# A state-space scan kernel whose side work is laid out anew over the items of a batch

## Chip, cores and metric

The kernel runs on one core of a Trainium2 chip. The metric is the device time of one execution in microseconds (us), the median of several runs. Engines are named as the profile names them: PE (TensorE), DVE (VectorE), ACT (ScalarE), POOL (GpSimd) and SP (SyncE, which only issues DMAs here).

## What is computed

The reference is a gated block of two parts over `x` of shape 4 x 512 x 512 (batch, time, channel). The first part is a selective state-space model over `ctx` (4 x 512 x 256), gated by the normalised `x`:

```python
x = einsum('bld,ed->bel', ctx, in_proj_w)              # 512 inner channels
x = silu(conv4(x) + conv_b)                            # causal, 4 taps, per channel
dt_low, B, C = split(einsum('bdl,ed->bel', x, x_proj_w), [16, 32])
dt = softplus(einsum('brl,dr->bdl', dt_low, dt_proj_w) + dt_proj_b)
# for each time step, with 16 states n for each channel d:
state = state * exp(dt * A) + (dt * x) * B
y = einsum('bdn,bn->bd', state, C)
y = (y + D * x) * silu(z)                              # z = layernorm of the block's x
x1 = x0 + tanh(g_xattn) * y.T
```

The second part is a layer norm and a mixture of 16 experts with top 2 of them and a shared expert, added to `x1`. The change does not touch it. All data is fp32.

## The kernel before

The scan part handles the four batches one after the other. A batch is 64 **items**: 16 steps `n` (one for each state), each with four groups `j` of 128 channels; item `i = 4n + j`. A batch's steps 0 and 1 stand in the tail of the batch before. A hardware loop runs over the first three batches (`b` = 0, 1, 2); the last batch is written out behind it. Each engine's program is written by hand as a sequence of items with semaphore waits, so the order on an engine is the order in the code, and nothing overtakes.

For each item the engines do the following, in this dependence:

- ACT (`decay`, L1161) writes `dA = exp(dt * A)` for the item into a ring of 8 slots; it may do so when the scan 8 items earlier is over, so ACT can be at most 8 items ahead. At `j == 2` it also writes the four input terms `dbuT` of the step (`input_terms`, L1172).
- PE (`step`, L766) transposes the item's quarter of `dbuT` into one of two PSUM banks `dbu_ps`; it may do so when the scan two items earlier is over, so PE is at most 2 items ahead.
- DVE (`scan`, L1474) runs the recurrence over 512 time steps into `hst`.
- POOL (`products`, L573) multiplies by the broadcast `C` row into `prod`, a ring of 4 slots.
- PE (`add_y`, L784) adds the product of the item five back into `y_ps`.

Between these stand the **pieces**, which prepare the next batch and finish the present one; they are chosen by `(n, j)` in a function `pieces` on each engine. They share two PSUM banks, `mp[0]` and `mp[1]`. Each use of a bank has a number: PE waits in `bank_free(k, use)` until the reader of the use before has counted up `misc_read[k]`, and signals `misc_full[k]`. `LOOP0` and `LOOP1` are the uses of each bank in a loop pass. The pieces are, in order:

- `in_proj` (two 128x512 matmuls into bank 1, for channel groups 3 and 1), whose result DVE folds with four taps (`conv`, L1421 and L1425);
- `conv_proj` (eight 128x512 matmuls for channel groups 0 and 2, the convolution folded into the weights, bank 0), copied by DVE (`conv_to_sbuf`, L1431);
- `z_transposes` (four transposes for one of four time tiles of the present batch's `silu(z)`, bank 0), copied and scaled by ACT (`z_to_time`, L1153);
- `ctx_transposes` of the batch after the next (bank 1), copied by DVE (`ctx_to_sbuf`);
- `silus` on ACT (L1121 and `silu_of_z`, L1114), with an activation table load ahead and one behind;
- `x_proj` (four matmuls, L727), its copy on DVE, `b_transposes` and the store of `C` to DRAM (`store_c` on SP);
- four rounds of `dt_proj` (L741), softplus on ACT (`softplus_parts`), a correction on DVE (`round_part`, L1450) and POOL (`log_part`, L554 and L557), the sum `dt_part` (L1456), `du_part` (L1467), `du_transposes` (L748, bank 1) and ACT's copy `du_to_time` (L1144);
- `post` on DVE at item 6 of the next batch: the gate by `zT`, the residual sum, then statistics (L1483 to L1490).

In the last batch only the z transposes are left as pieces of PE. ACT and DVE there also split the first weights of the second part into high and low halves (L1241, L1598, L1604).

## Time and profile before

| what | value |
|---|---|
| three timed runs | 1126.32, 1129.35, 1129.44 us; median 1129.35 us |
| the profiled execution | 1128.16 us, its span 1126.5 us |
| busy share of the span | PE 82%, PEld 69%, DVE 65%, ACT 54%, POOL 53% |
| mean granted TensorE clock | 0.916 of full |
| scan part | from the start to about 547 us of the span; loop batches of 121.7, 124.6 and 124.3 us from item 0 to item 0, the last batch 105.2 us |
| DMA | 137.08 MB, mean 122 GB/s |

Busy time is the time in which an instruction of the engine ran; a row's idle time is the engine's idle time just before the instructions of that row, put down to what ended it. In a timeline a row stands for one instruction or a run of equal ones (x count), with its start, its length and in brackets the idle time before it. One matmul of 128x512 in fp32 appears as two records. Since matmul records overlap, the pace of PE is read from one start to the next.

### The profile page before, as it was taken

To read this page: it belongs to the slowest core of one execution; us is meant where nothing else is said; L and a number is where in the kernel's file an instruction comes from. 1 tells how busy PE (TensorE), PEld (TensorE's weight loads), DVE (VectorE), ACT (ScalarE), POOL (GpSimd) and SP (SyncE) were. 2 spreads that over 40 slices of the span, in tenths; PEclk is the share of its full clock that TensorE was granted. 3 is DMA by queue.
4 is the path that set the end of the run, shared out by engine and by line. 5 is a ranking of instruction groups with operands and counts; after the bars stand their busy time and mean duration, and the time that the engine had idled before them with its cause. 6 is when DMAs were issued, how large, how long until landed. Compare 5 with 4: busy or idle time off the path is not lost.

```text
span 1126.5 us, 22746 instructions
## 1 busy us (share of the span) xinstructions
PE 926.3 (82%) x5388; PEld 781.1 (69%) x5389; DVE 731.2 (65%) x1023; ACT 613.7 (54%) x1037; POOL 592.3 (53%) x521
## 2 busy tenths in 40 slices
PE   6588977988788877677599989799999999883787
PEld 3266666766666656566489979699898888772676
DVE  4767789877987789599554458445454445444466
ACT  4687997679867987796122213334344445432211
POOL 4556797767966797699210005523434444431164
PEclk9579988998989989899699999989999999995699
DMA  7105111331105113111301015754556656563376
GB/s 250 39 21 186 58 29 39 130 103 31 40 34 184 50 35 108 38 51 35 106 28 47 37 48 168 284 190 162 192 188 228 226 183 227 190 220 112 107 228 236
DMA packets 67432, 137.08 MB, mean 122 GB/s; under 512 B 9392, under 2 KB 15024, under 8 KB 67248
## 3 DMA queue, kind: packets, MB, share of 16 engines
q1 hardware_dynamic: 54736, 105.66, 28.3%
q0 software_dynamic: 8960, 29.37, 7.3%
q10 hardware_dynamic: 3680, 1.39, 0.6%
q8 instruction: 24, 0.39, 0.1%
q14 instruction: 32, 0.26, 0.1%
HBM read 163.53 MB, written 42.07 MB: 183 GB/s over the span
## 4 chain that ended last, share of the span: by engine, by line
PE 39%; issue 4%; DVE 4%; POOL 3%; DMA 1%; ACT 1%; DVEq 0%; ACTq 0%; POOLq 0%
PE psY L955 12%; PE psG L919 11%; PE psU L919 10%; PE psT L912 3%; POOL slot_in L625 3%; PE psHT L933 2%; DVE x_tok L1864 1%; ACT xh L1288 1%; DMA gbuf<-slot_out,posi 0%; DVE hl L1676 0%; PE dbu_ps L766 0%; PE y_ps L784 0%; DVE xl L1682 0%; DVEq L1841 0%; POOL gbuf L672 0%
## 5 line engine op out<-in xcount | busy, mean ns | idle before, releaser
L573 POOL TENSOR_TENSOR prod<-hst,cbc 128x512 f32<-128x512 f32 x256 | 327.8, 1303 | 105.8 <-PE y_ps L784 94.4
L1474 DVE TENSOR_TENSOR_SCAN hst<-dA,dbu_ps 128x512 f32<-128x512 f32 x256 | 302.3, 1206 | 75.6 <-PE dbu_ps L766 57.8
L766 PE MATMUL dbu_ps<-ident,dbuT 128*128 128x128 f32 x1024 | 173.8, 296 | 61.4 <-DVE hst L1474 43.0
L766 PEld LDWEIGHTS dbu_ps<-ident,dbuT 128*128 128x128 f32 x1024 | 127.0, 151 | 127.9 <-DVE hst L1474 82.4
L1161 ACT ACTIVATE dA<-dts,Aneg 128x512 f32 (+1 forms) x256 | 172.6, 713 | 61.1 <-DVE hst L1474 60.4
L1294 ACT CAST hh<-psHT 128x384 fp32r<-128x384 f32 x79 | 37.8, 478 | 287.9 <-PE psHT L933 287.9
L1172 ACT ACTIVATE dbuT<-duT,BT 128x512 f32 (+1 forms) x256 | 163.0, 708 | 1.9 <-PE dbu_ps L766 1.9
L784 PE MATMUL y_ps<-ident,prod 128*128 128x128 f32 x1024 | 161.7, 285 | 1.3 <-POOL prod L573 1.3
L919 PE MATMUL psG<-weights,xh 128*128 (+1 forms) x560 | 140.9, 334 | 15.0 <-issue 8.7
L955 PE MATMUL psY<-weights,hh 128*128 (+3 forms) x420 | 136.3, 406 | 16.8 <-DVE hl L1676 14.6
L919 PE MATMUL psU<-weights,xh 128*128 (+2 forms) x560 | 142.7, 337 | 0.0
L784 PEld LDWEIGHTS y_ps<-ident,prod 128*128 128x128 f32 x1024 | 128.2, 149 | 2.0 <-POOL prod L573 2.0
L919 PEld LDWEIGHTS psG<-weights,xh 128*128 128x128 f32 x560 | 102.5, 195 | 25.2 <-issue 16.7
L660 POOL DMA_DIRECT2D slot_out<-yout x48 | 26.3, 547 | 171.4 <-DVE yout L1697 171.4
L1676 DVE TENSOR_TENSOR hl<-psHT,hh 128x384 fp32r<-128x384 f32 x80 | 44.4, 555 | 99.4 <-ACT hh L1294 99.0
L955 PEld LDWEIGHTS psY<-weights,hh 128*128 128x128 f32 (+1 forms) x420 | 77.6, 192 | 35.6 <-issue 12.1
L919 PEld LDWEIGHTS psU<-weights,xh 128*128 128x128 f32 x560 | 95.8, 191 | 0.0
L919 PE MATMUL psG<-weights,xl 128*128 (+1 forms) x280 | 93.0, 332 | 0.0
L919 PE MATMUL psU<-weights,xl 128*128 (+2 forms) x280 | 91.0, 325 | 0.0
L1241 ACT CAST weights<-raw_gu 128x704 f32 (+1 forms) x76 | 53.9, 778 | 55.8 <-DMA raw_gu<-in_L_ffn_w_gate_up_dram 29.4
L955 PE MATMUL psY<-weights,hl 128*128 (+3 forms) x210 | 83.1, 396 | 0.0
L1697 DVE COPY yout<-psY 128x512 f32<-128x512 f32 x48 | 33.2, 691 | 74.3 <-PE psY L955 65.5
(220 smaller groups left out, 1398.4 us busy)
## 6 DMA issues: line engine op xcount, KB each, us to landing
raw_gu<-in_L_ffn_w_gate_up_dram SPq DMA_DIRECT2D x100, 704.0 KB
raw_d<-in_L_ffn_w_down_dram SPq DMA_DIRECT2D x50, 512.0 KB
cbc<-c_rows SPq DMA_DIRECT2D x64, 256.0 KB, 3.1
slot_in<-ztile SPq DMA_DIRECT2D x3, 4096.0 KB, 13.6
gbuf<-slot_in SPq DMA_DIRECT2D x48, 256.0 KB, 3.1
slot_out<-yout POOLq DMA_DIRECT2D x48, 256.0 KB, 3.2
raw_d<-in_L_ffn_w_down_dram SPq DMA_DIRECT2D x50, 192.0 KB
xn_rows<-xin SPq DMA_DIRECT2D x16, 256.0 KB, 2.0
```

The costliest lines, as they stand in the source:

```text
L573: pool.tensor_tensor(prod[:, prod_slot(n, j), :], hst[:, slot_of(n, j), :], cbc[:, n % 2, :], ALU.mult).then_inc(prod_ready, 1)
L625: pool.indirect_dma_start(slot_in, bass.IndirectOffsetOnAxis(ap=posi[:, c, t:t + 1].bitcast(U32), axis=0), xn_kept_rows[:, t, :], None).th ...
L766: last = tr(dbu_ps[j % 2][:, t * P:(t + 1) * P], dbuT[:, n % 2, t, j * P:(j + 1) * P], ident[:])
L784: last = mm(y_ps[t][:, j * P:(j + 1) * P], prod[:, prod_slot(n, j), t * P:(t + 1) * P], ident[:], start=False, stop=m == ITEMS - 1, is_tra ...
L919: last = mm(ps[:, 0:width], a[:, k, c, :], w_at(w, buf)[:, c, w0:w0 + width], start=n == 0, stop=n == 3 * KH - 1)
L955: last = mm(psY[k][:], a[0:rows, k, c, :], w_at(w, buf)[0:rows, c, :], start=n == 0, stop=n == 8)
L1161: nc.scalar.activation(dA[:, slot_of(n, j), :], par(dts, b)[:, j, :], ACT.Exp, scale=Aneg[:, j, n:n + 1]).then_inc(da_ready, 1)
L1172: last = nc.scalar.activation(dbuT[:, n % 2, t, :], par(duT, b)[:, t, :], ACT.Copy, scale=par(BT, b)[:, t, RK + n:RK + n + 1])
L1241: nc.scalar.copy(dst(wgu_h)[:, c, 0:2 * INTER], raw_gu[:, c, :]).then_inc(gu_hi, 1)
L1294: nc.scalar.copy(hh[:, 1 - k, :, :], psHT[:, 0:3, :]).then_inc(hh_ready, 1)
L1474: V.tensor_tensor_scan(hst[:, slot_of(n, j), :], dA[:, slot_of(n, j), :], dbu_ps[j % 2][:], 0.0, ALU.mult, ALU.add).then_inc(scanned, 1)
L1676: V.tensor_tensor(hl[:, k, :, :], psHT[:, 0:3, :], hh[:, k, :, :].bitcast(F32), ALU.subtract).then_inc(hl_ready, 1)
```

## The change

The pieces get new places, counted in items from the batch's start:

| piece | before | after |
|---|---|---|
| `in_proj`, group 3 | both matmuls at item 9 | one each at 8, 9 |
| `conv_proj`, group 0 | 8 to 15 | 10 to 14, 17 to 19 |
| `in_proj`, group 1 | both at 18 | one each at 15, 16 |
| DVE's taps of group 3; group 1 | 11 to 14; 20 to 23 | 11 to 14; 17, 18, 19, 21 |
| `z_transposes` (PE) | 17, 19, 21, 23 on bank 0 | 23, 25, 27, 29 on bank 1 |
| `z_to_time` (ACT), loop | 24, 26, 28, 30 | 28, 30, 32, 34 |
| `z_transposes`, last batch | 17, 19, 21, 23 | 23, 25, 27, 29 |
| `z_to_time`, last batch | two after 27, two after 31 | 28, 30, 32, 34 |
| `conv_proj`, group 2 | 24 to 31 | 22, 24, 26, 28, 30 to 33 |
| `conv_to_sbuf`, group 0; 2 | 16; 32 | 20; 34 |
| `ctx_transposes`; copies | 32, 34; 33, 35 | 34, 36; 35, 37 |
| `silus` (ACT) | 39, `xs` first, then z | 40, z first, then `xs` |
| `x_proj`; copy on DVE | two each at 37, 38; 39 | one each at 37 to 40; 41 |
| `dt_proj` | 40, 44, 48, 52 | 42, 46, 50, 54 |
| `b_transposes`; copy | 40; 41 | 42; 43 |
| softplus on ACT | 48, 52, 56, 60 | 46, 50, 54, 58 |
| `round_part`; `dt_part`; `du_part` (first of four) | 42; 46; 47 | 44; 48; 49 |
| `log_part` on POOL (first of four) | 42 | 44 |
| `du_transposes` | 49, 53, 57, 61 | 50, 54, 58, 62 |
| `du_to_time` | 58, 62, 64, 65 | 57, 61, 64, 65 |

The uses of the banks change with it, and SP's load of `ctx` waits for bank 1's new count:

```diff
-        LOOP0, LOOP1 = 11, 9
+        LOOP0, LOOP1 = 7, 13
...
-                        sp.wait_ge(misc_full[1], base1(b) + 4)
+                        sp.wait_ge(misc_full[1], base1(b) + 8)
```

The order on PE, and the z transposes' bank:

```diff
             def z_transposes(use, b, t):
-                bank_free(0, use)
+                bank_free(1, use)
...
-                if 2 <= n < 4:
-                    conv_proj(0, base0(b), 0, m)
-                elif 6 <= n < 8:
-                    conv_proj(0, base0(b) + 5, 2, m)
-                if 4 <= n < 6 and j % 2 == 1:
-                    t = n % 2 * 2 + j // 2
-                    z_transposes(base0(b) + 1 + t, b, t)
-                if (n, j) == (2, 1):
-                    in_proj(1, base1(b), 3)
-                if (n, j) == (4, 2):
-                    in_proj(1, base1(b) + 1, 1)
...
+                i = n * ND + j
+                if i in (8, 9):
+                    in_proj(1, base1(b), 3, i - 8)
+                if 10 <= i < 15:
+                    conv_proj(0, base0(b), 0, i - 10)
+                if i in (15, 16):
+                    in_proj(1, base1(b) + 1, 1, i - 15)
+                if 17 <= i < 20:
+                    conv_proj(0, base0(b), 0, i - 12)
+                if i in (22, 24, 26, 28, 30, 31, 32, 33):
+                    conv_proj(0, base0(b) + 1, 2, (i - 22) // 2 if i < 30 else i - 26)
+                if i in (23, 25, 27, 29):
+                    z_transposes(base1(b) + 2 + (i - 23) // 2, b, (i - 23) // 2)
...
+                if 37 <= i < 41:
+                    x_proj(xp_use(bp), bp, i - 37, i - 36)
```

ACT's SiLUs, and its copies in the last batch:

```diff
             def silus(bp, conv_done):
+                silu_of_z(bp)
                 act.wait_ge(*conv_done)
                 nc.scalar.activation(xs[:].rearrange("p j l -> p (j l)"), xs[:].rearrange("p j l -> p (j l)"),
                                      ACT.Silu).then_inc(silu_done, 1)
-                silu_of_z(bp)
...
-                step(NB - 1, n)
-                if 6 <= n < 8:
-                    for t in range(n % 2 * 2, n % 2 * 2 + 2):
-                        z_to_time(NB - 1, t, base0(NB - 1) + t)
+                step(NB - 1, n, z_use=base1(NB - 1))
```

Two places of the built programs show the order. On PE, the loop batch's items 8 and 9 before (`dbu_ps` rows open an item, `mp` rows are its pieces, `winC` is a convolution matmul and `winT` an input projection):

```order
L766 MATMUL dbu_ps<-ident,dbuT 128x128 x4
L782 REGISTER_ALU
L784 MATMUL y_ps<-ident,prod 128x128 x4
L695 ISA
L717 MATMUL mp<-ctxT,winC 128x512
L764 REGISTER_ALU
L766 MATMUL dbu_ps<-ident,dbuT 128x128 x4
L782 REGISTER_ALU
L784 MATMUL y_ps<-ident,prod 128x128 x4
L717 MATMUL mp<-ctxT,winC 128x512
L695 ISA
L707 MATMUL mp<-ctxT,winT 128x512 x2
```

and the same two items now:

```order
L767 MATMUL dbu_ps<-ident,dbuT 128x128 x4
L783 REGISTER_ALU
L785 MATMUL y_ps<-ident,prod 128x128 x4
L695 ISA
L707 MATMUL mp<-ctxT,winT 128x512
L765 REGISTER_ALU
L767 MATMUL dbu_ps<-ident,dbuT 128x128 x4
L783 REGISTER_ALU
L785 MATMUL y_ps<-ident,prod 128x128 x4
L707 MATMUL mp<-ctxT,winT 128x512
```

Item 9 had three large matmuls behind its transposes and has one; the convolution starts two items later. On ACT, the last batch from the decays of step 6 on, before:

```order
L1161 ACTIVATE dA<-dts,Aneg 128x512
L1153 ACTIVATE zT<-mp,tg 128x512 x2
L1161 ACTIVATE dA<-dts,Aneg 128x512 x3
L1172 ACTIVATE dbuT<-duT,BT 128x512 x4
L1161 ACTIVATE dA<-dts,Aneg 128x512
L1153 ACTIVATE zT<-mp,tg 128x512 x2
```

and now:

```order
L1162 ACTIVATE dA<-dts,Aneg 128x512 x2
L1154 ACTIVATE zT<-mp,tg 128x512
L1162 ACTIVATE dA<-dts,Aneg 128x512 x2
L1173 ACTIVATE dbuT<-duT,BT 128x512 x4
L1154 ACTIVATE zT<-mp,tg 128x512
L1162 ACTIVATE dA<-dts,Aneg 128x512 x2
L1154 ACTIVATE zT<-mp,tg 128x512
L1162 ACTIVATE dA<-dts,Aneg 128x512 x2
L1173 ACTIVATE dbuT<-duT,BT 128x512 x4
L1154 ACTIVATE zT<-mp,tg 128x512
```

The two pairs of gate copies are now four single copies, each two items after the other, and PE's transposes for them stand six items later than they did.

## Rows read from the trace of the kernel before

**Rows 1.** The page's costliest groups: busy us, mean ns, idle before and its releaser.

```profile
L573 POOL TENSOR_TENSOR prod<-hst,cbc 128x512 f32<-128x512 f32 x256 | 327.8, 1303 | 105.8 <-PE y_ps L784 94.4
L1474 DVE TENSOR_TENSOR_SCAN hst<-dA,dbu_ps 128x512 f32<-128x512 f32 x256 | 302.3, 1206 | 75.6 <-PE dbu_ps L766 57.8
```

**Rows 2.** Windows: stretch, length, busy (x) of PE, PEld, DVE, ACT, POOL; granted clock, DMA, GB/s.

```profile
72.70:133.70 61.00, 55.01 (x331) 39.13 (x330) 46.09 (x46) 47.38 (x71) 42.92 (x35) 0.97 0.34 113
133.70:181.60 47.90, 36.56 (x222) 30.19 (x221) 40.21 (x37) 40.95 (x69) 43.35 (x33) 0.86 0.11 35
198.30:259.30 61.00, 55.01 (x330) 39.12 (x329) 46.04 (x45) 45.66 (x68) 42.85 (x34) 0.97 0.33 112
259.30:306.30 47.00, 35.50 (x223) 28.80 (x222) 40.55 (x39) 41.03 (x69) 43.18 (x33) 0.89 0.11 35
323.70:383.10 59.40, 53.41 (x331) 38.14 (x330) 46.09 (x46) 45.69 (x68) 42.77 (x34) 1.00 0.34 115
383.10:430.50 47.40, 34.36 (x222) 27.21 (x221) 39.70 (x37) 40.82 (x69) 43.20 (x33) 0.93 0.11 34
447.50:486.40 38.90, 28.41 (x201) 24.77 (x200) 26.72 (x35) 28.29 (x45) 29.28 (x24) 0.87 0.12 35
486.40:537.20 50.80, 37.58 (x275) 30.70 (x273) 47.85 (x41) 38.69 (x63) 47.18 (x36) 0.97 0.13 42
```

**Rows 3.** Timeline of DVE, second loop batch: start, length, instruction, idle before.

```profile
198.28 1.22 DVE L1474 TENSOR_TENSOR_SCAN hst<-dA,dbu_ps 128x512 f32<-128x512 f32 x1
...
207.04 1.21 DVE L1474 TENSOR_TENSOR_SCAN hst<-dA,dbu_ps 128x512 f32<-128x512 f32 x1
...
208.81 1.21 DVE L1474 TENSOR_TENSOR_SCAN hst<-dA,dbu_ps 128x512 f32<-128x512 f32 x1
...
228.03 1.21 DVE L1474 TENSOR_TENSOR_SCAN hst<-dA,dbu_ps 128x512 f32<-128x512 f32 x1
232.03 1.22 DVE L1474 TENSOR_TENSOR_SCAN hst<-dA,dbu_ps 128x512 f32<-128x512 f32 x1 [2.79 <-PE dbu_ps L766]
```

**Rows 4.** Timeline of PE in the same batch, steps 6 and 7.

```profile
229.64 1.50 PE L717 MATMUL mp<-ctxT,winC 128*128 128x512 f32 x2 [2.78 <-ACT zT L1153]
...
235.75 0.60 PE L766 MATMUL dbu_ps<-ident,dbuT 128*128 128x128 f32 x4
...
236.62 1.02 PE L717 MATMUL mp<-ctxT,winC 128*128 128x512 f32 x2
237.49 0.60 PE L766 MATMUL dbu_ps<-ident,dbuT 128*128 128x128 f32 x4
```

**Rows 5.** Timeline of ACT in the same batch, around the SiLUs.

```profile
246.75 1.28 ACT L1121 ACT_TABLE_LOAD   x1
...
249.86 2.91 ACT L1114 ACTIVATE zs<-x_tok,rs 128x512 f32 x4
...
258.39 2.54 ACT L1161 ACTIVATE dA<-dts,Aneg 128x512 f32 x4
```

**Rows 6.** Timelines of PE and DVE in the last batch, steps 4 and 5.

```profile
465.41 1.11 PE L756 MATMUL mp<-ident,zs 128*128 128x128 f32 x4 [4.94 <-ACT zT L1153]
...
467.47 1.22 DVE L1474 TENSOR_TENSOR_SCAN hst<-dA,dbu_ps 128x512 f32<-128x512 f32 x1 [5.75 <-issue]
...
478.42 1.22 DVE L1474 TENSOR_TENSOR_SCAN hst<-dA,dbu_ps 128x512 f32<-128x512 f32 x1 [5.49 <-issue]
```

**Rows 7.** Timeline of ACT in the last batch, steps 8 and 9.

```profile
482.98 2.55 ACT L1172 ACTIVATE dbuT<-duT,BT 128x512 f32<-128x512 f32 x4
...
488.57 2.55 ACT L1172 ACTIVATE dbuT<-duT,BT 128x512 f32<-128x512 f32 x4
```

**Rows 8.** Timelines of POOL and DVE, second loop batch, from step 10 on.

```profile
270.30 5.15 POOL L573 TENSOR_TENSOR prod<-hst,cbc 128x512 f32<-128x512 f32 x4
...
278.81 5.17 POOL L573 TENSOR_TENSOR prod<-hst,cbc 128x512 f32<-128x512 f32 x4
...
300.58 4.54 DVE L1474 TENSOR_TENSOR_SCAN hst<-dA,dbu_ps 128x512 f32<-128x512 f32 x4
```

More of the change, by code:

```diff
@@ L574, in products @@
                                        ALU.mult).then_inc(prod_ready, 1)
-                    if bp is not None and 10 <= n < 14 and j == 2:
-                        log_part(bp, n - 10)
+                    if bp is not None and 11 <= n < 15 and j == 0:
+                        log_part(bp, n - 11)
             for j in range(ND):
@@ L702, in ctx_transposes, with in_proj @@
                 last.then_inc(full, 1)
-            def in_proj(k, use, j):
-                bank_free(k, use)
-                for c in range(NK):
-                    last = mm(mp[k][:], winT[:, c, j * P:(j + 1) * P], ctxT[:, c, PADC:PADC + L],
-                              start=c == 0, stop=c == NK - 1)
-                last.then_inc(misc_full[k], 1)
+            def in_proj(k, use, j, c):
+                if c == 0:
+                    bank_free(k, use)
+                last = mm(mp[k][:], winT[:, c, j * P:(j + 1) * P], ctxT[:, c, PADC:PADC + L],
+                          start=c == 0, stop=c == NK - 1)
+                if c == NK - 1:
+                    last.then_inc(misc_full[k], 1)
             def conv_proj(k, use, j, m):
@@ L755, in z_transposes @@
                 for j in range(ND):
-                    last = tr(mp[0][:, j * P:(j + 1) * P], zs[:, j, t * P:(t + 1) * P], ident[:])
-                last.then_inc(misc_full[0], 1)
+                    last = tr(mp[1][:, j * P:(j + 1) * P], zs[:, j, t * P:(t + 1) * P], ident[:])
+                last.then_inc(misc_full[1], 1)
             def step(b, n, j):
@@ L882, in _ @@
                     add_y(NB - 1, n * ND + j - LAG)
-                    if 4 <= n < 6 and j % 2 == 1:
-                        t = n % 2 * 2 + j // 2
-                        z_transposes(base0(NB - 1) + t, NB - 1, t)
+                    if n * ND + j in (23, 25, 27, 29):
+                        t = (n * ND + j - 23) // 2
+                        z_transposes(base1(NB - 1) + t, NB - 1, t)
             for m in range(ITEMS - LAG, ITEMS):
@@ L1152, in z_to_time @@
                     act.sem_inc(wait_carrier, 1)
-                nc.scalar.activation(zT[:, t, :], mp[0][:], ACT.Copy, scale=tg[:, 0:1]).then_inc(misc_read[0], 1)
+                nc.scalar.activation(zT[:, t, :], mp[1][:], ACT.Copy, scale=tg[:, 0:1]).then_inc(misc_read[1], 1)
             def decay(b, n, j):
@@ L1174, in input_terms, with step @@
                 last.then_inc(dbut_ready, 1)
-            def step(b, n, bp=None):
+            def step(b, n, bp=None, z_use=None):
                 for j in range(ND):
@@ L1182, in step @@
                         pieces(bp, n, j)
+                    t = (n * ND + j - 28) // 2
+                    if z_use is not None and j % 2 == 0 and 0 <= t < NL:
+                        z_to_time(b, t, z_use + t)
             def pieces(bp, n, j):
                 b = bp - 1
-                if 6 <= n < 8 and j % 2 == 0:
-                    t = n % 2 * 2 + j // 2
-                    z_to_time(b, t, base0(b) + 1 + t)
-                if (n, j) == (9, 3):
-                    silus(bp, (misc_read[0], base0(b) + 7))
-                if 12 <= n < 16 and j == 0:
-                    softplus_parts(bp, n - 12)
-                if 14 <= n < 16 and j == 2:
+                i = n * ND + j
+                if i in (28, 30, 32, 34):
+                    t = (i - 28) // 2
+                    z_to_time(b, t, base1(b) + 2 + t)
+                if i == 40:
+                    silus(bp, (misc_read[0], base0(b) + 3))
+                if 11 <= n < 15 and j == 2:
+                    softplus_parts(bp, n - 11)
+                if 14 <= n < 16 and j == 1:
                     du_to_time(bp, n - 14)
```

76 lines of the change are left out of this document (35 added, 41 removed).

## The prediction

> **What bounds the kernel now.** I read the page first: over the span no engine is full, so the share of busy time decides nothing. The costliest groups are POOL's products and DVE's scans, and both idle mostly behind PE [rows 1]. Then I cut the scan part into windows [rows 2]. A loop batch falls into two stretches. In the first, from item 8 to 40 (61.0, 61.0 and 59.4 us), PE is busiest, with 55.0 of 61.0 us, at a granted clock near 1; in the second, from item 40 to the next batch's item 0 (47.9, 47.0 and 47.4 us), POOL is, with 43.2 to 43.4 us. Third, the timelines tell the pace of an item, and the reader is to see three of them.
>
> - PE alone: a new item's transposes start at 235.75, its large matmul at 236.62 and the next item at 237.49 [rows 4]. So transposes and products cost 0.87 us and one large matmul ("a pass") 0.87, 1.74 together. A z or ctx transpose piece is four small transposes, half of that 0.87, so such an item costs 1.31.
> - DVE: a scan alone paces at 1.13 (a run of four is 4.54 long) [rows 8]; with a tap or copy out of PSUM behind it, 1.77, from 207.04 to 208.81 [rows 3].
> - POOL from step 10 on: 8.51 us a step (270.30 to 278.81), 5.15 of it four products, the rest two logarithm corrections [rows 8].
>
> DVE's tap (1.77) hides PE's pass (1.74) in the same item. PE may lead DVE by two items only, so two passes too many in one item aren't absorbed: they are paid in full, while a single pass in an item without DVE work costs 1.74 - 1.13 = 0.61. That is what the new layout plays on. Two real waits stand out besides. In the loop PE waits 2.78 us for ACT's last gate copy before the second convolution (229.64), and runs on at half clock: that matmul row is 1.50 long against 1.02 at full clock [rows 4]. In the last batch PE waits 4.94 us and DVE 5.75 and 5.49 us at two places, for the gate copies again [rows 6]. All four z transposes share a bank with a reader that stands up to ten items further on.
>
> **Part by part.** The working is against the profiled execution, 1128.16 us (1.2 under the median).
>
> *Items 8 to 24, loop.* Before, 198.28 to 228.03, 29.8 us [rows 3]. After: items 8, 9, 10 are PE's, 3 x 1.74 = 5.2; 11 to 14 have a tap each, 4 x 1.77 = 7.1; 15 and 16 (one projection matmul each) 3.3, because the first has to wait for the bank until the tap of item 14; 17 to 21 have DVE work each, 5 x 1.77 = 8.9; 22 and 23 cost 1.13 each, as PE has caught up where item 20 and 21 had none of its work. Sum 26.7, a gain of 3.1. Bounds: 1 (the lead is not regained) to 4.
>
> *Items 24 to 40, loop.* Before, 31.3 us in the second batch. After: 24 and 25 at 1.4 (PE is still a little ahead), 26 to 29 alternate 1.74 and 1.31, 6.1; 30 to 33 are 4 x 1.74 = 7.0; 34 and 35 carry DVE copies, 3.5; 36 costs 1.2. That puts item 37's scan 20.6 us behind item 24's. ACT decides the rest. Its unit costs: four decays or a step's four input terms are 2.55 long as a run and, less the overlap with what follows, 2.45, so 0.61 each; a gate copy is of the same size and taken alike; a table load is 1.28, the load and `xs`'s SiLU 3.11 together (246.75 to 249.86), the z SiLUs 2.9 [rows 5, 7]. Count from the end of scan 20. ACT, eight items ahead, does decay 28 and waits for PE's transposes in item 23, done at 3.3; then until the decay of item 40 stand 12 decays (7.4), three sets of input terms (7.4) and four copies (2.4): 20.5. Load and z SiLUs: 24.7; `xs`'s SiLU (1.83): 26.5. PE wants it for item 37's `x_proj` at about 25.4, so it waits 1 us, scan 38 starts 2.9 behind scan 37, 39 another 1.7. The second table load, two decays and the input terms of step 10 end at 31.4, item 40 follows 2.3 behind 39. Sum 20.6 + 6.9 = 27.5, a gain of 3.8. The half-clock stretch goes with the wait. Bounds: 0 (ACT late by 4 more) to 6 (no wait for the SiLU). The order of the SiLUs alone costs: before, `xs` was ready 3.1 behind its wait, now the z SiLUs come first; only ACT's idle time until the second convolution pays for them.
>
> The Trainium skill ("ScalarE: Activation LUTs", What ACT_TABLE_LOAD costs) counts a switch of sets at about 2.66 us, since it puts a drain of 1.38 behind the load; here load and SiLU of 2048 elements take 3.11 together, and less the load's 1.28 only 1.83 are left for the SiLU itself, so the trace does not agree. By the page both switches would be 1.38 longer, item 40 up to 2.8 later in each loop batch, and the sum below 8 us smaller.
>
> *Item 40 to the next batch, loop.* Everything moves two items back, and the round of one step stays: POOL's 8.51 binds. `round_part` now stands four items nearer the front against ACT's softplus (item 44 against 46, formerly 42 against 48), so its waits for the exponentials go: I price that at 2 to 3 us, the idle time that POOL's rate leaves to be won on DVE (47.0 us against the 43.2 that POOL works). Against it, `log_part` starts two items later (2.3), and the last `du_part` is at item 61: formerly it ended just before the scan of 300.58, and the next batch's first scan came at 306.3, 5.7 us later, through the transposes, ACT's copy, a decay and four input terms [rows 2, 8]. Behind item 61 there are 2 scans of 1.13 to hide it instead of 4, so the chain shows 3.4 us where it showed 1.1. But from the last correction to the end there are two scans fewer, 2.3 us, so that end stays as long as it was. Net I take 46.0 us against 47.4 on the mean, between 45 and 51 (all 2.3 + 2.2 lost, no wait won).
>
> Loop batches: 26.7 + 27.5 + 46.0 = 100.2 against 108.9, 108.0 and 106.8: gains of 8.7, 7.8 and 6.6, together 23.
>
> *Last batch.* The two stalls are DVE's 5.75 and 5.49 [rows 6]. Now PE's transposes at 23 + 2t stand five items ahead of ACT's copy, and the next transposes need ACT past item 28 + 2t, three items ahead of PE: it has six or seven. PE's items alternate between 1.31 and 0.87, 1.09 on the mean, under DVE's 1.13: hidden. So 11.2 us would go; but ACT, which caught up in the stalls, is full: it works 5.59 us a step from step 8 on (482.98 to 488.57) [rows 7] and in the window with the stalls it works 28.3 of 38.9 us, which without 11.2 us of stall is full [rows 2]. Carried on without stalls, its input terms of step 10 come 9 us earlier, not 11. I take 9, bounds 5 and 12.
>
> *Queues passed.* SP's `load_ctx` waits for PE's item 36 instead of 34, with the `C` row of step 10 queued behind it; that row may only be loaded once product 35 is done, which is later, so nothing. `store_c` waits for item 41 instead of 39, ahead of the row of step 12, likewise. The second part starts from DVE's end of the scan part and moves with it.
>
> Sum: 1128.2 - 23 - 9 = 1096. New runs should scatter as the old did, up to 1.2 above the profiled one: **1097**.
>
> **Rivals.**
>
> - *The loop's gain is given back behind item 40.* POOL is the bound there with 43 of 47 us [rows 2]. If the two later items and the longer turn to the next batch are paid in full (4.5 a batch) and the waits for exponentials stay, a loop batch gains 7.8 - 5.9 = 1.9, three of them 6, with the last 15: 1113. For it: POOL has no slack. Against: POOL itself waited for the first correction.
> - *ACT becomes late for bank 1: slower.* The z transposes and ACT's copies now share bank 1, one copy per two items, while ACT also carries decays. Should ACT's lead over PE fall under three items at item 25, PE stands in front of `bank_free`, everything behind it on PE too, and the stalls of the last batch [rows 6] stay there and appear in the loop: 3 x 11.2 = 34 more, against 3 x 4.5 won elsewhere: 1128 + 34 - 13 = 1149. It decides from a lead of three; before, ACT is limited by its ring of eight in most of these items, which speaks against it.
> - *The layout moves passes but their cost stays.* If PE's passes were hidden already wherever they stood, only the last batch gains: 1119. Against: PE's 55 of 61 us.
>
> **How the numbers follow.** Forecast 0.76; given back 0.11; only the last batch 0.05; lost in the noise 0.03 (a measurement of this kernel can tell about 0.3%, 3.4 us); slower 0.05. The forecast's own bounds: loop 3 x (1 + 0 - 3.5) to 3 x (4 + 6 + 2.5), last 5 to 12; taken together and not all at one end, 1084 to 1111. Reaching to the first rival: **1084 to 1115**. Faster 0.92, same 0.03, slower 0.05.
>
> **What would show it.** In the changed profile, items 8 to 24 should take near 27 us and 24 to 40 near 28; no PE wait on `zT` over 1 us; a wait of about 1 us on `xs` before `x_proj`; 46 us behind item 40, with a stall near 3 us before the next batch; the last batch without idle of 5 us on DVE, and ACT full in it. I am wrong if PE waits at `bank_free` for `zT`, if `x_proj` waits over 4 us, or if the windows behind item 40 grow by over 3 us.

## The result and the profile after

The changed kernel takes 1106.42 us on the median of four runs (1105.03 to 1107.3), the kernel before 1127.84 us beside it (1121.5 to 1129.44): the ratio is 0.9826, with a 95% interval from 0.9803 to 0.985. The profiled execution took 1106.53 us, with a span of 1104.9 us against 1126.5. The scan part, from the first scan's start to the last one's end, fell from 475.8 to 453.5 us; all that lies behind it takes 591.4 us instead of 590.8. So the whole gain of the profiled execution, 22.3 us, lies in the scan part.

The page's costliest groups of the kernel after (busy us, mean ns, idle before and its releaser) answer to [rows 1]:

```profile
L573 POOL TENSOR_TENSOR prod<-hst,cbc 128x512 f32<-128x512 f32 x256 | 333.0, 1327 | 84.8 <-PE y_ps L785 66.9
L1476 DVE TENSOR_TENSOR_SCAN hst<-dA,dbu_ps 128x512 f32<-128x512 f32 x256 | 304.0, 1208 | 67.8 <-PE dbu_ps L767 57.8
```

POOL waits 21 us less and DVE 8; POOL's 256 products have themselves become 5.2 us longer in sum. Where the time went is read from the scans' start times on DVE. Each number is the distance between two scans, in the three loop batches one after the other, and the last batch:

| items | before | after | forecast |
|---|---|---|---|
| 0 to 8 | 12.8, 16.7, 17.5; 17.0 | 13.4, 18.2, 16.8; 18.5 | not priced |
| 8 to 24 | 29.8, 29.8, 29.8 | 27.0, 27.0, 27.0 | 26.7 |
| 24 to 40 | 31.2, 31.3, 29.6 | 28.4, 28.4, 28.4 | 27.5 |
| 40 to 44 | 8.5, 9.3, 8.5 | 7.4, 7.4, 7.4 | |
| 44 to 61 | 34.9, 33.1, 34.4 | 33.6, 33.5, 33.7 | |
| 61 to next 0 | 4.5, 4.6, 4.5 | 7.2, 7.2, 7.2 | |
| 40 to next 0 | 47.9, 47.0, 47.5 | 48.1, 48.1, 48.2 | 46.0 |
| last batch, 8 to end | 88.2 | 76.1 | 79.2 |

Items 8 to 40 give 5.6, 5.7 and 4.0 us, 15.2 together; what lies behind item 40 takes back 2.0; the last batch from item 8 on gives 12.2; the items 0 to 8 take back 3.1 (sums taken before rounding). Together that is the 22.3.

The windows of the second and the last batch of the kernel after (length, busy us and instructions of PE, PEld, DVE, ACT, POOL, then the granted clock, the DMA share and GB/s) answer to [rows 2]:

```profile
195.10:222.00 26.90, 26.50 (x163) 18.86 (x162) 24.32 (x25) 17.05 (x27) 21.89 (x18) 1.00 0.44 157
222.00:250.40 28.40, 25.68 (x168) 18.64 (x167) 21.16 (x20) 28.13 (x42) 20.46 (x17) 1.00 0.29 92
250.40:257.80 7.40, 6.82 (x46) 4.55 (x44) 5.51 (x6) 6.23 (x11) 4.59 (x4) 1.00 0.17 40
257.80:291.40 33.60, 24.95 (x160) 20.41 (x161) 30.94 (x30) 30.21 (x51) 33.03 (x25) 0.90 0.09 31
291.40:298.50 7.10, 2.63 (x22) 2.17 (x21) 4.09 (x5) 4.45 (x8) 6.56 (x5) 1.00 0.15 38
...
437.50:466.30 28.80, 25.80 (x204) 21.66 (x203) 27.59 (x36) 26.32 (x43) 28.80 (x24) 1.00 0.15 48
466.30:513.50 47.20, 34.80 (x268) 28.67 (x267) 44.08 (x40) 39.57 (x65) 44.87 (x35) 1.00 0.16 45
```

The stretches now have a nearly full engine, another one each time: PE with 26.50 of 26.9 us in items 8 to 24, ACT with 28.13 of 28.4 in 24 to 40, PE again with 6.82 of 7.4 in 40 to 44, POOL with 33.03 of 33.6 in 44 to 61. The half-clock stretch of [rows 4] is gone: the granted clock is 1.00 from item 8 to 44. In the turn (items 61 to the next 0, the last line of the batch) POOL works 6.56 of 7.1 us, where it worked all of 4.6.

The same cut through the kernel before, second batch, from item 24 on:

```profile
228.00:259.30 31.30, 27.93 (x158) 19.18 (x159) 21.52 (x21) 24.96 (x36) 19.78 (x16) 0.95 0.24 68
259.30:268.60 9.30, 8.14 (x44) 6.14 (x42) 6.21 (x7) 9.27 (x16) 6.05 (x6) 0.82 0.13 32
268.60:301.70 33.10, 24.45 (x156) 20.21 (x156) 30.88 (x29) 27.25 (x46) 32.53 (x24) 0.90 0.09 32
301.70:306.30 4.60, 2.92 (x23) 2.45 (x24) 3.46 (x5) 4.52 (x8) 4.60 (x5) 1.00 0.19 59
```

In items 40 to 44 ACT was full, 9.27 of 9.3 us, and POOL was not. In 44 to 61 POOL was as full as it is now, 32.53 of 33.1 us. The prediction had not cut these lines out, and they decide what lies behind item 40.

### The profile page after: what moved, and what is told of

The parts are those of the page before. It is cut to its first block, busy times and chain, and to the rows that moved or that the text cites. A ratio compares the mean times of both kernels' runs of the same rounds, so it can differ in the third digit from the quotient of the medians.

```text
span 1104.9 us, 22746 instructions
## 1 busy us (share of the span) xinstructions
PE 920.2 (83%) x5388; PEld 776.6 (70%) x5389; DVE 728.1 (66%) x1023; ACT 611.2 (55%) x1037; POOL 594.0 (54%) x521
## 4 chain that ended last, share of the span: by engine, by line
PE 40%; issue 4%; DVE 4%; POOL 3%; DMA 1%; ACT 1%; DVEq 0%; POOLq 0%
PE psY L956 12%; PE psG L920 11%; PE psU L920 10%; PE psT L913 3%; POOL slot_in L625 3%; PE psHT L934 3%; DVE x_tok L1864 1%; ACT xh L1290 1%; DMA gbuf<-slot_out,posi 0%; PE dbu_ps L767 0%; DVE hl L1676 0%; DVEq L1841 0%; DVE xl L1682 0%; PE y_ps L785 0%; POOL gbuf L672 0%
## 5 line engine op out<-in xcount | busy, mean ns | idle before, releaser
L573 POOL TENSOR_TENSOR prod<-hst,cbc 128x512 f32<-128x512 f32 x256 | 333.0, 1327 | 84.8 <-PE y_ps L785 66.9
L767 PE MATMUL dbu_ps<-ident,dbuT 128*128 128x128 f32 x1024 | 169.9, 292 | 38.5 <-ACT dbuT L1173 16.8
L1162 ACT ACTIVATE dA<-dts,Aneg 128x512 f32 (+1 forms) x256 | 169.3, 712 | 33.2 <-DVE hst L1476 32.7
L956 PE MATMUL psY<-weights,hh 128*128 (+3 forms) x420 | 135.7, 405 | 16.7 <-DVE hl L1676 14.3
L1697 DVE COPY yout<-psY 128x512 f32<-128x512 f32 x48 | 33.2, 692 | 73.8 <-PE psY L956 65.8
```

The source lines that it names most:

```text
L573: pool.tensor_tensor(prod[:, prod_slot(n, j), :], hst[:, slot_of(n, j), :], cbc[:, n % 2, :], ALU.mult).then_inc(prod_ready, 1)
L767: last = tr(dbu_ps[j % 2][:, t * P:(t + 1) * P], dbuT[:, n % 2, t, j * P:(j + 1) * P], ident[:])
L956: last = mm(psY[k][:], a[0:rows, k, c, :], w_at(w, buf)[0:rows, c, :], start=n == 0, stop=n == 8)
L1162: nc.scalar.activation(dA[:, slot_of(n, j), :], par(dts, b)[:, j, :], ACT.Exp, scale=Aneg[:, j, n:n + 1]).then_inc(da_ready, 1)
L1697: ins = V.tensor_copy(yout[:, k, :], psY[k][:])
```

## The experiments

All kernels ran beside the kernel before on the same chip. There were three sets: in the first (e1 to e4) that kernel took 1153.12 us, in the second (e5 to e8) 1127.86, in the third (e10, e11 and the changed kernel again) 1149.92. The changed kernel's scan part was 453.5 us in its first profile and 453.6 in the third set, so for it the 22 us more of the third lie behind the scan part; the kernel before was profiled only once. So between sets the stretches are compared, and the ratios within one. The stretches of each kernel come from one profiled execution, and its ratio from four runs, if nothing else is said.

**The changed kernel once more (c_after_again).**

> The changed kernel itself, once more, for the scatter of its stretches. Ratio to before 0.980 to 0.985. If the stretches behind item 40 are set by the order of the program, they come out as in the first look: 24 to 40 28.4, 40 to 64 48.1 us in each loop batch, within 0.3. If the excess of 0.6 to 1.5 us in the items 0 to 8 belongs to the changed kernel (as it would if the longer turn before them were its cause), items 0 to 8 take 13.4, 18.2, 16.8, 18.5 again; if it is scatter from run to run, they differ by a microsecond or more in one batch at least, and need not lie above the 12.8, 16.7, 17.5, 17.0 of before.

Measured: ratio 0.9864 [0.984, 0.9888], above what was expected: 22.3 us of 1149.92 would be 0.981. The scan part has its 453.6 us; what lies behind it took 613.1 us here, and between 613.1 and 619.0 in the three profiles of this set, for the same instructions. That part was not studied, and why it scatters more there is open. Items 8 to 44 came out to 0.1 us (27.0, 28.4, 7.4). Behind item 40 it was 48.5, 48.1 and 51.0: the third is 2.8 longer, so the scatter there is larger than expected. Items 0 to 8 took 12.2, 17.0, 18.5, 17.6, other values in other batches: they don't belong to the changed kernel as such. They go with the granted clock of the stretch. Three windows of items 0 to 8 of the kernel before, then three of the changed one (first profile), show it in the last but two column:

```profile
181.60:198.30 16.70, 11.53 (x83) 10.15 (x82) 16.27 (x21) 14.64 (x24) 10.19 (x11) 0.90 0.10 33
306.30:323.80 17.50, 12.34 (x83) 10.95 (x82) 16.28 (x21) 14.57 (x24) 10.81 (x12) 0.80 0.09 30
430.50:447.50 17.00, 11.83 (x84) 10.45 (x83) 16.27 (x21) 14.65 (x24) 10.25 (x11) 0.90 0.48 158
```

```profile
176.90:195.10 18.20, 13.78 (x83) 12.86 (x82) 16.36 (x21) 14.56 (x24) 10.58 (x11) 0.72 0.09 30
298.50:315.40 16.90, 11.74 (x83) 10.35 (x82) 16.29 (x21) 14.63 (x24) 10.19 (x11) 0.90 0.10 32
419.00:437.50 18.50, 14.08 (x84) 13.16 (x83) 16.47 (x21) 14.57 (x24) 10.79 (x11) 0.72 0.44 145
```

At 0.90 the eight items take 16.7 to 17.0 us, at 0.80 17.5 and at 0.72 18.2 to 18.5, for the same instructions. What makes the clock differ was not tested. In all of them PE first waits 3.5 us for DVE's gates, and DVE then waits for PE; its rows tell at which clock it caught up. The twelve small matmuls before item 8 take 2.35 us in the first of these windows of the changed kernel and 1.55 in the second:

```profile
192.25 2.35 PE L785 MATMUL y_ps<-ident,prod 128*128 128x128 f32 x12
...
313.35 1.55 PE L785 MATMUL y_ps<-ident,prod 128*128 128x128 f32 x12
```

**Only the last batch's gate copies spread (e1_last_only).** The kernel before, with the last batch's z transposes at 23, 25, 27, 29 and copies at 28, 30, 32, 34, still on bank 0:

```diff
-                    if 4 <= n < 6 and j % 2 == 1:
-                        t = n % 2 * 2 + j // 2
+                    if n * ND + j in (23, 25, 27, 29):
+                        t = (n * ND + j - 23) // 2
                         z_transposes(base0(NB - 1) + t, NB - 1, t)
```

> The kernel before, with the new places of the gate transposes (items 23 to 29) and of ACT's four copies (28 to 34) in the last batch alone, on the old bank. If the last batch's part of the change stands by itself, item 8 of that batch to its last scan shortens by 12 us, as it did in the changed kernel (88.2 to 76.1), and the whole run is about 1116; the three loop batches stay at 121.7, 124.6 and 124.3. Rival: that part needs the other bank or comes with the loop's new phase; then it gains under 6 us and the run is above 1121.

Measured: ratio 0.9919 [0.989, 0.9948]. The last batch took 76.2 us from item 8 on, as in the changed kernel, so its 12 us are the spread alone and owe nothing to the bank: over half of the whole gain. The profile shows a second thing: here the loop is the kernel before's, and yet it took 46.1, 46.2 and 46.2 us behind item 40, not 47.9, 47.0 and 47.5. The base from which the prediction reckoned was long by 1.3 us a batch of scatter there (in the first batch items 24 to 40 were 1.4 us longer in turn, 32.6).

**The late pieces put back (e5_late_as_before).** The changed kernel with `x_proj` in pairs at 37 and 38, and `dt_proj`, softplus, corrections, `du_part` and their transposes at their former items:

```diff
-                if 37 <= i < 41:
-                    x_proj(xp_use(bp), bp, i - 37, i - 36)
-                if 10 <= n < 14 and j == 2:
+                if 37 <= i < 39:
+                    x_proj(xp_use(bp), bp, (i - 37) * 2, (i - 36) * 2)
+                if 10 <= n < 14 and j == 0:
...
-                if 12 <= n < 16 and j == 1:
-                    du_part(bp, n - 12)
+                if 11 <= n < 15 and j == 3:
+                    du_part(bp, n - 11)
```

> The changed kernel up to item 36, with everything from x_proj on at the items of the kernel before (x_proj two and two at 37 and 38, dt_proj at 40, softplus at 48, corrections from 42, the last du_part at 59). Theory A: the late pieces' new places lost what the forecast missed behind item 40; then the stretch from 40 stays at 46 to 47.5 us, the turn's idle on DVE is 1.1 instead of 2.9 us, item 40 comes no later than 28.4 us behind item 24 (ACT's input terms set it, not x_proj), and a loop batch is 1 to 3 us shorter than in the changed kernel: ratio to the kernel before 0.974 to 0.980. Rival: doubling x_proj's passes costs what the later places lose, or POOL sets the pace whatever the places; then the batch stays within 1 us of the changed kernel's and the ratio is 0.981 or above.

Measured: ratio 0.9778 [0.9762, 0.9795], the best of its set; the scan part is 448.3 us, 5.2 less than with the whole change. Theory A gave the ratio rightly, but not where: items 24 to 40 went from 28.4 to 29.7, which it had ruled out, and from 40 to the next batch it was 45.6, 45.4 and 45.5 instead of 48.1 (7.9, 33.1 and 4.5 in the three stretches, instead of 7.4, 33.6 and 7.2). The turn made the difference. On DVE, the turn of the changed kernel and then that of this one:

```profile
292.49 0.66 DVE L1469 TENSOR_TENSOR du<-dts,xs 128x512 f32<-128x512 f32 x1
293.07 2.55 DVE L1476 TENSOR_TENSOR_SCAN hst<-dA,dbu_ps 128x512 f32<-128x512 f32 x2
298.52 1.22 DVE L1476 TENSOR_TENSOR_SCAN hst<-dA,dbu_ps 128x512 f32<-128x512 f32 x1 [2.90 <-PE dbu_ps L767]
```

```profile
288.15 0.66 DVE L1469 TENSOR_TENSOR du<-dts,xs 128x512 f32<-128x512 f32 x1
288.74 4.54 DVE L1476 TENSOR_TENSOR_SCAN hst<-dA,dbu_ps 128x512 f32<-128x512 f32 x4
294.42 2.33 DVE L1476 TENSOR_TENSOR_SCAN hst<-dA,dbu_ps 128x512 f32<-128x512 f32 x2 [1.14 <-PE dbu_ps L767]
```

From the last `du` to the next batch's first scan it is 6.0 us with two scans under it and 6.3 with four. The chain is of one length; what counts is how many scans lie over it. Two scans are 2.3 us, and the turn is longer by 2.6.

**`du_part` an item earlier (e2_du_part_early).** Only `du_part` moves, from the second to the first item of its step, to shorten that chain:

```diff
-                if 12 <= n < 16 and j == 1:
+                if 12 <= n < 16 and j == 0:
                     du_part(bp, n - 12)
```

> The changed kernel, with DVE's du_part one item earlier (48, 52, 56, 60, right behind dt_part). Theory A: what the loop lost behind item 40 is PE's wait for du (2.6, 2.0, 2.9 and 1.4 us in a batch), the half clock it leaves behind, and the long chain over the last du at the turn of the batch (2.9 us idle on DVE). Then the stretch from item 40 to the next batch shrinks from 48.1 to about 46.5, the turn's idle from 2.9 to 1.8, and the run is 1100 to 1103. Theory B: POOL's 8.7 us a step binds the stretch; then items 40 to 60 take as long as before and only the turn gains 1.1 a batch or nothing, 1103 to 1106.

Measured: ratio 0.9873 [0.984, 0.9906], against 0.9839 and 0.9824 for the two other edits of its set; the turn fell from 7.2 to 5.5 us, but items 44 to 61 rose from 33.6 to 39.7, 38.4 and 38.4, which neither theory had. DVE's and POOL's rows in this kernel:

```profile
265.69 5.61 POOL L573 TENSOR_TENSOR prod<-hst,cbc 128x512 f32<-128x512 f32 x4
...
268.41 1.75 DVE L1458 TENSOR_TENSOR dts<-sp_r,sp_l 128x512 f32 x1
270.41 1.44 DVE L1469 TENSOR_TENSOR du<-dts,xs 128x512 f32<-128x512 f32 x1 [0.24 <-DVE dts L1458]
...
279.50 1.71 POOL L554 TENSOR_TENSOR sp_t<-sp_t,sp_u 128x512 f32<-128x512 f32 x1
...
278.33 1.76 DVE L1458 TENSOR_TENSOR dts<-sp_r,sp_l 128x512 f32 x1
280.27 1.49 DVE L1469 TENSOR_TENSOR du<-dts,xs 128x512 f32<-128x512 f32 x1 [0.18 <-DVE dts L1458]
```

The same `du` product takes 0.66 us behind a scan and 1.44 here; in all 12 of them 16.8 us against 7.9. These 8.9 us are 3.0 of the 5 us that a batch lost in items 44 to 61 by the move; the rest was not taken apart. In the changed kernel the rows were:

```profile
263.49 5.62 POOL L573 TENSOR_TENSOR prod<-hst,cbc 128x512 f32<-128x512 f32 x4
269.07 1.75 POOL L554 TENSOR_TENSOR sp_t<-sp_t,sp_u 128x512 f32<-128x512 f32 x1
...
269.02 0.66 DVE L1469 TENSOR_TENSOR du<-dts,xs 128x512 f32<-128x512 f32 x1
```

The slow `du` starts 0.89 us before POOL's running product ends (270.41 against 271.30), the fast one 0.09 us before (269.02 against 269.11), and then POOL's next instruction is the long one, 1.75 us. It is so for all of them: the 12 fast ones start 0.1 us before the end of POOL's instruction, and the next one of POOL takes 1.75 to 1.77 us; the 12 slow ones start 0.5 to 0.9 us before it and take 1.06 to 1.50. The Trainium skill ("SBUF — State Buffer", Who interferes with whom) says that a DVE instruction with two SBUF inputs contends with a GpSimd instruction that reads SBUF, and that the order of issue decides which of the two is blocked. The trace agrees: whichever starts second is the longer one.

**The transposes of `du` an item later (e3_du_tr_late).** In the changed kernel PE stood at the `du` transposes for `du_part` in every step, 2.56, 1.97, 2.90 and 1.44 us in the second batch. This edit takes the wait away:

```diff
-                if 12 <= n < 16 and j == 2:
+                if 12 <= n < 16 and j == 3:
                     du_transposes(dut_use(bp) + n - 12, bp, n - 12)
```

> The changed kernel, with PE's transposes of du one item later (51, 55, 59, 63). It takes PE's wait for du away but leaves DVE alone and makes the chain at the turn of the batch one item longer. Theory A, with the turn's chain as the costlier half: the turn's idle grows from 2.9 to 4.0 us, items 44 to 60 gain under 1 us, and the run is 1106 to 1110. Rival: PE's waits and its half clock in items 48 to 60 are what costs; then the stretch from 40 shortens by 1 us or more a batch and the run is 1101 to 1104.

Measured: ratio 0.9839 [0.9814, 0.9865]. Items 44 to 61 stayed at 33.5, 33.5 and 33.5 us though PE no longer waits for `du`, and the turn grew to 7.8, 9.1 and 9.1 us, as theory A had it: the last transposes are on its chain. The three waits in the middle cost nothing: POOL is the bound and PE has slack. The fourth is the turn.

**The former order of the SiLUs (e4_xs_first).** `xs` first, then z:

```diff
-                silu_of_z(bp)
                 act.wait_ge(*conv_done)
...
                                      ACT.Silu).then_inc(silu_done, 1)
+                silu_of_z(bp)
```

> The changed kernel, with ACT's SiLU of xs ahead of the z SiLUs again, as in the kernel before, still at item 40. Theory A (ACT's order matters little, one wait replaces the other): the scan of item 38 comes 1.5 to 2 us earlier, as x_proj no longer waits 1.6 us, and item 40 waits longer for its input terms by 0.5 to 1; a loop batch changes by -1.3 to 0 us and the run is 1103 to 1106. Rival (the new order was needed because ACT has no idle time to give): ACT's wait for the second convolution stands open now, input terms of steps 10 and 11 come over 2 us late, and the run is 1108 or more.

Measured: ratio 0.9824 [0.9802, 0.9845]; items 24 to 40 28.4 us as before the edit. The wait moved and kept its size. In the changed kernel PE waits 1.59 us for `xs` before the first `x_proj`:

```profile
244.58 1.06 PE L728 MATMUL mp<-xs,xpT 128*48 128x512 f32 x2 [1.59 <-ACT xs L1123]
...
246.59 1.06 PE L728 MATMUL mp<-xs,xpT 128*48 128x512 f32 x2
```

and with `xs` first it waits 1.78 us for the input terms of step 10, two items later:

```profile
242.96 1.06 PE L728 MATMUL mp<-xs,xpT 128*48 128x512 f32 x2
...
247.81 0.65 PE L767 MATMUL dbu_ps<-ident,dbuT 128*128 128x128 f32 x4 [1.78 <-ACT dbuT L1173]
```

Scan 38 came 2.01 us behind scan 37 instead of 3.67, scan 40 3.86 behind 39 instead of 2.17. ACT is full, so whichever of its results is asked for first is late.

**Both, the late pieces put back and `xs` first (e10_late_xs_first).** The edits of e5_late_as_before and e4_xs_first together.

> The changed kernel with all that stands from x_proj on where it was before (as in e5_late_as_before) and with xs's SiLU ahead of the z SiLUs. Theory: in e5_late_as_before the 29.7 us of items 24 to 40 hold 1.3 us of waiting for xs, which the pair of x_proj chunks in item 37 pays at once and which nothing behind takes up; with xs ready about 2.9 us earlier that goes until ACT's input terms of step 10 set item 40, as they did in e4_xs_first: 24 to 40 28.4, a loop batch 1.3 shorter, in all 4 us less than e5_late_as_before, ratio 0.974. Rival: the pair of chunks itself costs the 1.3 (two x_proj chunks in one item are more than PE's lead of two items holds), whichever SiLU comes first: 24 to 40 stays at 29.7, ratio 0.978.

Measured: ratio 0.9829 [0.9807, 0.985], 0.9971 of the changed kernel's median on the same chip. Items 24 to 40 fell to 28.4 as the theory had it, but 40 to 44 rose from 7.9 to 8.5, 9.2 and 9.3: in the second and third batch nothing was gained up to item 44, in the first 0.7 us. The theory stopped at item 40, and ACT's work does not. Its table load behind the SiLUs and the row that stands behind the end of DVE's wait for `sp_u` (the next one of the softplus), first with z first, in e5_late_as_before, and then with `xs` first, in e10_late_xs_first:

```profile
241.80 1.28 ACT L1125 ACT_TABLE_LOAD   x1
...
254.71 0.63 ACT L1141 ACTIVATE sp_l<-sp_u 128x512 f32<-128x512 f32 x1
```

```profile
244.13 1.28 ACT L1125 ACT_TABLE_LOAD   x1
...
257.04 0.63 ACT L1141 ACTIVATE sp_l<-sp_u 128x512 f32<-128x512 f32 x1
```

Between the two rows lie 12.91 us in each. Scan 24 started at 219.30 and 221.63, so the load came 22.50 us behind it in both, and the softplus row 35.41. Up to DVE's first correction, in item 42, only what ACT has to do before it counts, and the order of the SiLUs decides merely in which items the same time shows. The correction waits for it on DVE:

```profile
257.04 1.11 DVE L1452 TENSOR_SCALAR sp_t<-sp_u 128x512 f32<-128x512 f32 x1 [1.42 <-ACT sp_u L1139]
```

In the changed kernel the same row of ACT stands 35.44 us behind scan 24, but the correction stands two items later and doesn't wait: items 40 to 44 take 7.4 us. So this late place is worth 1.1 to 1.9 us against e10_late_xs_first. e10_late_xs_first and e5_late_as_before still differ by 0.6 to 1.5 us in 44 to 61, in which nothing was edited; what makes that is open.

**The gate copies three items later (e6_copies_later).** ACT's copies at 31, 33, 35, 37 instead of 28, 30, 32, 34:

```diff
-                if i in (28, 30, 32, 34):
-                    t = (i - 28) // 2
+                if i in (31, 33, 35, 37):
+                    t = (i - 31) // 2
```

> The changed kernel, with ACT's four gate copies three items later, at 31, 33, 35, 37 in every batch; PE's transposes stay. It tests from which distance the shared bank bites. PE at item 25 + 2t then needs ACT past item 31 + 2t, six items ahead, where it was three. Theory A: it bites at that distance: PE waits over 0.5 us for zT at two or three of the transposes and before the first ctx transpose, items 24 to 40 grow from 28.4 to 31 or more, and the last batch gets its stalls back (76.1 us from item 8 becomes 80 or more); ratio 0.990 to 1.005. Rival: ACT's lead of eight covers it; all stretches within 0.5 us, ratio about 0.983.

Measured: ratio 0.9889 [0.9869, 0.9909] (two runs only), just under the range of theory A. Items 24 to 40 took 29.3 instead of 28.4 us, the last batch from item 8 on 81.5 instead of 76.1, and PE stands in front of the bank again. The waits on `zT` in the whole program, in this kernel (who waited, us, times), and in the changed one:

```profile
  PEld mp L757: 13.0, 8
  POOL dA L580: 11.2, 4
  PE mp L757: 11.1, 8
```

```profile
  PEld mp L757: 1.1, 1
  DVE dA L1556: 0.9, 1
  PE mp L757: 0.9, 1
```

This is the mechanism of the rival that ended slower. The copies at five items' distance are clear of it, those at eight are not, and even then it costs 10.5 us of the scan part (464.0 against 453.5), not the 34 that the rival gave it: the loop pays 0.9 us a batch in 24 to 40, up to 2.9 behind 40, where the unchanged program scattered by 2.8, and 5.4 in the last batch. No kernel put the z transposes of the loop back to their old items or bank, so how the gain of items 24 to 40 divides between those two is not shown.

**`in_proj` in pairs again (e7_in_proj_doubled).** Both matmuls of a pair at item 9 and at 16 (the second edit is like the first):

```diff
-                if i in (8, 9):
-                    in_proj(1, base1(b), 3, i - 8)
+                if i == 9:
+                    in_proj(1, base1(b), 3, 0)
+                    in_proj(1, base1(b), 3, 1)
```

> The changed kernel, with both matmuls of each input projection in one item again (9 and 16), and none in 8 and 15. Theory A (a pass alone costs 1.74 - 1.13 = 0.61 us, a second one in the same item its full 0.87, since PE leads by two items only): items 8 to 24 take 27.5 us instead of 27.0, three times, 1.5 us in all, which only the trace can tell. Rival: PE's lead takes it up, and the stretch stays at 27.0 or falls.

Measured: ratio 0.9799 [0.978, 0.9819] (two runs only); items 8 to 24 26.8 us instead of 27.0: the rival held. Item 8 takes 1.14 and item 9 2.33 us where both took 1.73, item 15 1.13 and 16 2.14. The sums are 3.47 against 3.46 and 3.27 against 3.47: a pair in one item, with a free one ahead, costs what two single ones cost. PE's lead of two items takes it up. So spreading the two matmuls of a pair did not bring the 2.8 us of this stretch. What differs from the kernel before is that there item 9 held three passes, the pair and one of the convolution, and took 3.45 us, and that three z transposes, at 17, 19 and 21, stood among the taps. No kernel divides the gain between the two, but the scans' distances in the second batch do by place: 1.6 us of it lie in items 8 to 16, all in item 9, and 1.2 in 17 to 23.

**The turn filled (e8_turn_filled).** ACT's last `du_to_time` of a batch behind the decay of item 2 of the next batch instead of ahead of it (the old call at `j == 1` goes, which is not shown):

```diff
                     decay(b, n, j)
+                    if j == 2 and n == 0 and bp is not None:
+                        du_to_time(bp, 3)
                     if j == 2:
                         input_terms(b, n)
```

> The changed kernel, with ACT's last du_to_time of a batch behind the decay of item 2 of the next batch instead of ahead of it, so that this decay runs while ACT waits for PE. Theory A: the chain du_part, PE's transposes, ACT's copy, input terms, PE's transposes sets the next batch's item 0, and the decay stands in it with 0.6 us: DVE's idle at the turn falls from 2.9 to 2.3 us, 1.8 us in all, more if PE keeps its clock. Rival: something else (POOL's products) sets that item; then it doesn't move.

Measured: ratio 0.9802 [0.9784, 0.982]; the turn 7.0 instead of 7.2 us, a third of the 0.6 expected. The stall on DVE fell from 2.90 to 2.70. That decay was mostly not on the chain.

**All together (e11_best).** e10_late_xs_first, with `in_proj` in pairs and the turn filled.

> All that has helped or cost nothing, together: e10_late_xs_first, with each projection matmul pair of in_proj in one item again (9 and 16), and du_to_time(3) put between the scans of the next batch's items 1 and 2. Theory: pieces add, so loop batches take 27.0 to 26.8 us in items 8 to 24, 28.4 in 24 to 40, 45.3 in 40 to 64; ratio 0.973 to 0.975. Rival: e7_in_proj_doubled's 0.2 us came only because slack followed, and moving the copy at the turn pushes du_to_time behind the scan that ACT's decay chain waits for, now that the turn has only 1.1 us of stall: the turn grows by about 0.6 us a batch and the ratio is that of e10_late_xs_first or 0.001 to 0.002 above it.

Measured (six runs): ratio 0.9782 [0.9751, 0.9812], 0.9915 of the changed kernel's median on the same chip; the scan part 448.7 us, against 448.3 of e5_late_as_before. Stretches 26.8, 28.4, then 47.3, 47.2 and 46.8 behind item 40. Neither the theory's 45.3 behind item 40 nor the rival's longer turn came (it fell to 4.4). It does not beat e5_late_as_before (0.9778 in its own set); both are ahead of the changed kernel, by under 1%.

## Why the prediction was right, and where not

The forecast was 1097 us with a range from 1084 to 1115; measured 1106.42. Direction and places held; the loop's gain was overrated: 13.2 us from item 8 on instead of 23. That the total still came within 10 us owes something to luck: the last batch gave 3.2 us more than forecast, and items 0 to 8, which stood in no sum, took 3.1.

- **Items 8 to 24: right in the sum.** 26.7 forecast, 27.0 measured. Items 8 to 10 at 1.73 each and those with a tap at 1.77 are the paces of [rows 3, 4]. The rule given, that two passes too many in an item are paid in full, stands for item 9 of before (three passes, 3.45 us); for a pair alone it does not: e7_in_proj_doubled shows that it costs nothing with a free item ahead of it.
- **Items 24 to 40: right in mechanism, 0.9 us short.** Scan 37 came 20.55 us behind scan 24 (forecast 20.6). Then 3.67, 2.01 and 2.17 instead of 2.9, 1.7 and 2.3. The wait for `xs` was 1.59 us instead of 1, and an item with `x_proj` takes 2.01 us and not 1.74: `x_proj`'s two rows lie 2.01 apart. ACT is the bound, as the forecast said, and e4_xs_first and e10_late_xs_first show that the order of its SiLUs only moves the wait.
- **Item 40 to the next batch: the step that failed.** Forecast 46.0, measured 48.1, three times 2.1. Both terms were seen, the waits and the turn, and their sum was wrong.
  - The waits. "Its waits for the exponentials go" came true: DVE waited 1.15, 1.50 and 0.34 us for `sp_u` in the second batch before (in all 3.0; 3.9 and 4.7 in the two others), and never in the changed kernel. They were priced at 2 to 3 us, out of the distance between 47.0 and POOL's 43.2. That idle time of POOL lay ahead of item 44. There the first of the waits was indeed worth something: items 40 to 44 take 7.4 us instead of 8.5, 9.3 and 8.5, and e10_late_xs_first, with the correction at its old item, has 8.5 to 9.3 again. The later waits lay in items 44 to 61, where POOL was full already, and were worth nothing: e5_late_as_before has them again (1.0 to 1.7 us in item 46) and takes 33.0 to 33.2 us there against 33.6.
  - The turn. 3.4 us of stall were forecast and 2.90 measured, but "that end stays as long as it was" took it out of the sum again. It was paid in full: the turn is 7.2 us instead of 4.5, and with the pieces at their old items (e5_late_as_before) 4.5 again. The prediction let the same two scans, 2.3 us, pay both for the later `log_part` and for the longer chain. Its terms as they stand, 2 to 3 us won, 2.3 and 2.3 lost, 2.3 won, lead from 47.4 to between 46.7 and 47.7, not to 46.0.
  - The base was long by 1.3 us of scatter besides, as e1_last_only shows: against its 46.2 the change loses 1.9 us a batch here.
- **POOL's round of 8.51: 8.70 now.** Twelve products of `dt` on DVE took 19.0 us instead of 17.6, and 36 of POOL's products take over 1.35 us where 19 did. This is the 5.2 us in the page's POOL row. With the late pieces put back the POOL row reads 327.1 us again, so the place of those pieces makes it. Most of it is no new work: POOL's corrections (L554, L557) took 33.5 us instead of 37.1, and all of POOL's work 594.0 instead of 592.3. What DVE's products cost POOL falls on other instructions now.

```profile
263.49 5.62 POOL L573 TENSOR_TENSOR prod<-hst,cbc 128x512 f32<-128x512 f32 x4
...
272.19 5.60 POOL L573 TENSOR_TENSOR prod<-hst,cbc 128x512 f32<-128x512 f32 x4
```

- **Last batch: right, and 3 us more.** 12.2 instead of 9; the stalls of [rows 6] are gone. ACT was priced as full; it works 26.32 of 28.8 us and then 39.57 of 47.2, so it held the batch back at some items only. DVE's longest waits there are now 1.2 and 1.6 us, for ACT's decays:

```profile
461.82 4.55 DVE L1476 TENSOR_TENSOR_SCAN hst<-dA,dbu_ps 128x512 f32<-128x512 f32 x4 [1.21 <-ACT dA L1162]
...
473.02 4.55 DVE L1476 TENSOR_TENSOR_SCAN hst<-dA,dbu_ps 128x512 f32<-128x512 f32 x4 [1.60 <-ACT dA L1162]
```

- **Items 0 to 8: not priced.** 3.1 us went with the granted clock of this execution, as far as the windows show; the second profile of the same kernel (c_after_again) had 1.4 of it.

The difference adds up: 0.8 for items 8 to 24, 2.7 for 24 to 40, 6.4 behind item 40, 3.1 for items 0 to 8, 0.6 behind the scan part, less 3.2 for the last batch, makes 10.4, against 10.3 between 1096.2, which is the forecast for the profiled execution, and its 1106.53. Of the rivals, the first named the right place and half of the way: the longer turn is paid, but the waits for the exponentials did not stay. It gave 4.5 us a batch against the 2.6 of e5_late_as_before. On the table load: the Trainium skill ("ScalarE: Activation LUTs", What ACT_TABLE_LOAD costs) would have made the switches longer than the trace has them; after the change load and z SiLUs begin at 238.50 and 239.79, 1.29 us apart, and the first decay follows the second load after 1.30, so the trace again does not agree.

## What to carry to other kernels

Cut the time into stretches short enough that one engine is full in each, and ask in each whether the wait that is removed belongs to that engine. A wait that goes on another engine than the full one is worth nothing (DVE's for the exponentials behind item 44 here, with POOL full), a wait in a stretch that hangs on it is worth something (the first of them, in items 40 to 44, where 1.1 to 1.9 us a batch were won), and the price of one must not be taken from idle time that lies in a neighbouring stretch. Where a chain crosses the turn between two rounds, count the work left to lie over it: moving everything two items back looks neutral and exposes two items of it. Count each scan that hides something once. And when an engine is full, as ACT is here from item 24 to 40, reordering its work only moves the wait; what would shorten the stretch, less work or the same work where the engine has room, was not tried here.
